# Linear attention on one core: queries, keys and values projected in one run, the gate's projection between the state's two chunks, the numerators last in a tile

## The reference

```
q = phi(rope(x @ Wq + bq)); k = phi(rope(x @ Wk + bk))      # 16 heads of 16; phi = elu + 1
v = x @ Wv + bv;            g = sigmoid(x @ Wg + bg)
for each chunk of 64 tokens:
    S = S + k_c^T v_c;      Z = Z + sum(k_c)
    out_c = g_c * (q_c S) / (q_c Z + 1e-6)
x = x + out @ Wo + bo                                        # x is rms-normed before the projections
```

## Time and profile before

| | |
|---|---|
| median of 3 runs | 1467.9 us (1464.53 to 1470.61) |
| profiled execution | 1477.02 us, its span 1475.2 us |
| PE busy in the span | 1422.5 us, 96% |
| PEld / DVE / ACT / POOL busy | 93% / 68% / 49% / 53% |
| mean granted TensorE clock | 0.976 |
| attention phase in the trace | 0 to about 226 us |

### The profile page before, as it was taken

How to read it: one execution, slowest core, us unless ns; L and a number is a source line. 1 busy time by engine, 2 the same in 40 slices (tenths; PEclk the granted TensorE clock), 3 DMA queues, 4 the chain that set the end, 5 groups by cost and what they waited for, 6 DMA issues and landing times. The chain is left out here.

```text
span 1475.2 us, 36261 instructions
## 1 busy us (share of the span) xinstructions
PE 1422.5 (96%) x11761; PEld 1373.3 (93%) x11761; DVE 1008.9 (68%) x2860; ACT 717.1 (49%) x1793; POOL 776.7 (53%) x792
## 2 busy tenths in 40 slices
PE   8999995999999999999969999999999999999997
PEld 7888884999999999999958999999999999999997
DVE  6999986666677667667685656666566656566685
ACT  4776664555555545555553434444344434443353
POOL 3677751566666666666442444344443444343477
PEclk9999996999999999999978999999999999999999
DMA  7121223343343442443443142313323132321442
GB/s 269 44 72 41 66 72 86 97 106 52 94 102 49 105 102 43 101 101 76 88 173 111 29 122 36 115 29 75 75 33 117 29 114 36 114 36 29 114 146 86
DMA packets 63560, 124.79 MB, mean 85 GB/s; under 512 B 14336, under 2 KB 51840, under 8 KB 60416
## 3 DMA queue, kind: packets, MB, share of 16 engines
q0 software_dynamic: 35936, 47.89, 18.9%
q1 hardware_dynamic: 27552, 76.02, 14.2%
HBM read 80.97 MB, written 42.90 MB: 84 GB/s over the span
## 5 line engine op out<-in xcount | busy, mean ns | idle before, releaser
L926 POOL DMA_INDIRECT mg<-meta,IDX x160 | 151.0, 944 | 307.0 <-DVE E_gate L1278 280.6
L1364 DVE TENSOR_TENSOR E_hraw<-E_sg,bank 128x256 f32<-128x256 f32 x320 | 133.2, 417 | 242.1 <-ACT E_sg L1212 191.7
L1061 POOL DMA_INDIRECT acc<-ysb,IDX x150 | 241.5, 1610 | 77.6 <-issue 48.6
L1434 PE MATMUL bank<-E_xT,ws 128*128 128x256 f32 x960 | 267.6, 279 | 3.9 <-ACT E_hraw L1215 2.5
L1435 PE MATMUL bank<-E_xT,ws 128*128 128x256 f32 x960 | 265.6, 277 | 0.0
L1436 PE MATMUL bank<-E_xT,ws 128*128 128x256 f32 x960 | 265.6, 277 | 0.0
L1375 DVE TENSOR_TENSOR E_hT<-E_hraw,E_hT 128x256 fp32r<-128x256 f32 x640 | 259.9, 416 | 0.0
L1371 DVE CAST E_hT<-E_hraw 128x256 fp32r<-128x256 f32 x640 | 203.1, 318 | 78.7 <-ACT E_hraw L1215 72.2
L1212 ACT ACTIVATE E_sg<-bank 128x256 f32<-128x256 f32 x320 | 116.0, 382 | 240.0 <-PE bank L1436 228.7
L1434 PEld LDWEIGHTS bank<-E_xT,ws 128*128 128x128 f32 x960 | 180.5, 188 | 7.6 <-ACT E_hraw L1215 5.3
L1434 PE MATMUL bank<-ws,E_hT 128*128 128x256 f32 x640 | 180.6, 282 | 0.0
(11 more groups left out here) (238 smaller groups left out, 3938.8 us busy)
## 6 DMA issues: line engine op xcount, KB each, us to landing
wraw<-in_w_ffn SPq DMA_DIRECT2D x8, 3072.0 KB, 10.8
wraw<-in_w_moe SPq DMA_DIRECT2D x8, 2048.0 KB, 12.2
acc<-x SPq DMA_DIRECT2D x32, 128.0 KB, 1.7
xn<-xn SPq DMA_DIRECT2D x32, 128.0 KB, 1.7
acc<-X POOLq DMA_DIRECT2D x4, 1024.0 KB, 9.0
acc<-X SPq DMA_DIRECT2D x8, 512.0 KB, 4.2
X<-acc SPq DMA_DIRECT2D x7, 512.0 KB, 5.9
X<-in_x SPq DMA_DIRECT2D x3, 1024.0 KB, 11.9
```

Of the source, the lines that this page charges most:

```text
L926: nc.gpsimd.indirect_dma_start(out=mg[:, j, 0:width], out_offset=None, in_=rows, in_offset=bass.IndirectOffsetOnAxis(ap=IDX[:, u * UT + j: ...
L1061: nc.gpsimd.indirect_dma_start(out=acc_dram, out_offset=at_slots(u, j), in_=ysb[:, j, :], in_offset=None, compute_op=ALU.add).then_inc(s_y ...
L1364: V.tensor_tensor(hraw[:, f % RING, :], sg[:, f % RING, :], bank[f % RING][:, UW:2 * UW], ALU.mult).then_inc(s_hm, 1)
L1434: nc.tensor.matmul(out, wh, mh, start=first, stop=False)
```

## The change

Only the order of blocks in TensorE's `step` changes, with each block's own waits. Every instruction, operand, bank and semaphore count is the same, and the other engines' programs are as before.

- before: P0, turn, tq, S0, V, S1, to, G, num, wo
- after: P0, V, turn, tq, to, S0, G, S1, wo, num

```diff
@@ TensorE's step
                     project(n, b_p0[:, :], half_a).then_inc(s_pj0, 1)
+                if (n := at(1)) is not None:
+                    if n == 0:
+                        pe.wait_ge(s_wl, 3 * KD)
+                    after(pe, s_vf, n)
+                    project(n, b_pv[:, 0:D], slice(2 * D, 3 * D)).then_inc(s_pjv, 1)
                 if (n := at(2)) is not None and n:
                     turn(n)
...
                     ins.then_inc(s_tq, 1)
-                    pe.wait_ge(s_vz, 2 * n + 1)
-                    after(pe, s_mk, 2 * n)
-                    add_chunk(n, 0)
-                if (n := at(1)) is not None:
-                    if n == 0:
-                        pe.wait_ge(s_wl, 3 * KD)
-                    after(pe, s_vf, n)
-                    project(n, b_pv[:, 0:D], slice(2 * D, 3 * D)).then_inc(s_pjv, 1)
-                if (n := at(0)) is not None:
-                    pe.wait_ge(s_mk, 2 * n + 1)
-                    pe.wait_ge(s_vz, 2 * n + 2)
-                    add_chunk(n, 1)
                 if (n := at(-1)) is not None:
                     pe.wait_ge(s_og, n + 1)
                     after(pe, s_oT, n)
...
                     ins.then_inc(s_to, 1)
+                if (n := at(0)) is not None:
+                    pe.wait_ge(s_vz, 2 * n + 1)
+                    after(pe, s_mk, 2 * n)
+                    add_chunk(n, 0)
                 if (n := at(1)) is not None:
                     after(pe, s_gt, n)
                     after(pe, s_lx, n)
                     project(n, b_pg[:, 0:DX], slice(3 * D, WX)).then_inc(s_pjg, 1)
+                if (n := at(0)) is not None:
+                    pe.wait_ge(s_mk, 2 * n + 1)
+                    pe.wait_ge(s_vz, 2 * n + 2)
+                    add_chunk(n, 1)
                 if t == -1:
                     turn_weights()
+                if (n := at(-1)) is not None:
+                    pe.wait_ge(s_oT, n + 1)
+                    pe.wait_ge(s_qT, min(n + 2, NT))
+                    after(pe, s_x1, n)
...
                     ins.then_inc(s_num, 1)
-                if (n := at(-1)) is not None:
-                    pe.wait_ge(s_oT, n + 1)
-                    pe.wait_ge(s_qT, min(n + 2, NT))
-                    after(pe, s_x1, n)
...
```

More of the change, by code:

```diff
@@ L647, in step @@
                     project(n, b_pg[:, 0:DX], slice(3 * D, WX)).then_inc(s_pjg, 1)
+                if (n := at(0)) is not None:
+                    pe.wait_ge(s_mk, 2 * n + 1)
+                    pe.wait_ge(s_vz, 2 * n + 2)
+                    add_chunk(n, 1)
                 if t == -1:
                     turn_weights()
+                if (n := at(-1)) is not None:
+                    pe.wait_ge(s_oT, n + 1)
+                    pe.wait_ge(s_qT, min(n + 2, NT))
+                    after(pe, s_x1, n)
+                    for k in range(KD):
+                        ins = nc.tensor.matmul(wo_ps, oT[:, k, :], wo[:, k, :], start=(k == 0), stop=(k == KD - 1))
+                    ins.then_inc(s_wo, 1)
                 if (n := at(0)) is not None:
@@ L660, in step @@
                     ins.then_inc(s_num, 1)
-                if (n := at(-1)) is not None:
-                    pe.wait_ge(s_oT, n + 1)
-                    pe.wait_ge(s_qT, min(n + 2, NT))
-                    after(pe, s_x1, n)
-                    for k in range(KD):
-                        ins = nc.tensor.matmul(wo_ps, oT[:, k, :], wo[:, k, :], start=(k == 0), stop=(k == KD - 1))
-                    ins.then_inc(s_wo, 1)
             run_tiles(pe, step)
```

## The result

The changed kernel takes 1477.3 us in the median of 7 runs, 1467.9 before; the ratio is 1.0074 with a 95% interval of 1.0053 to 1.0096. A second series (`after_again`), beside runs of its own of the kernel before, gave 1476.8 against 1464.8, ratio 1.0087 (1.0065 to 1.0109). So it is slower by 0.5 to 1.1%. The forecast was 1476.0 us, +8.1.

What follows compares the result with a forecast made beforehand. TensorE was taken as the bound, with small waits. Tile 6.12 + 0.54 = 6.66 us against 6.41, +0.25; 30 tiles give 7.5, with the end 8.1; 1467.9 + 8.1 = 1476.0 us, range 1465 to 1483.

Steps and rivals of the forecast that it cites:

- G's wait on the copy: In each attention tile, TensorE's G waits for ScalarE's copy of 8 logit columns: +0.54 us (0.38 to 0.72).
- The 0.15 from copy to matmul: From the logit copy's end to G's first matmul, a wait on two semaphores, taken as 0.15 us.
- What the new order takes away: In each attention tile, TensorE loses waits of 0.16 and 0.12 and another 0.02: 6.12 us without any new wait.
- two waits of TensorE (0.16 and 0.12): Old order, per tile: S1's wait on mask 0 with a bare load, 0.16 us; num's second half behind mask 1, 0.12.
- The first rival: G finds the logit copy done: tile 6.12 us, whole kernel 1459.8 us, faster; chance 0.1.
- The third rival: ScalarE falls behind in the attention tiles, slower still: 1480.5 to 1484 us; chance 0.15.
- Phi: At the start of VectorE's step: its move was put at nothing, with some 0.5 us to spare before mask 0.
- The ends: Start and end of the attention phase: 0 us (-0.8 to +0.8) and +0.6 us (0 to 0.8).
- The weight loads: On TensorE, loads are hidden behind matmuls in flight, bare after a wait (0.10 us); the skill's rule would give 3 us more.

Runs made afterwards that it cites:

- e11: The kernel before with tq and S0 moved ahead of turn (the input's transposes): 1469.0 us against 1464.8, ratio 1.0028.
- e4: The kernel before with only wo and num swapped at the tile's end: 1477.8 us against 1464.7, ratio 1.0096.

## Why the prediction was right, step by step

- **G's wait on the copy.** Right in mechanism, place and size. Forecast: S0 at 2.85 after P0, G at 3.79, tile 6.66, +0.25; measured 2.86, 3.80, 6.68 and +0.27. Moving the copy earlier took the wait away, moving it later lengthened the tile, and in the old order an early copy was worth nothing.
- **The 0.15 from copy to matmul.** It was 0.14, and 0.06 with G's two waits written in the other order.
- **What the new order takes away.** Right for this kernel, wrong as a floor. S1 and num wait for no mask there only because G's wait gives the masks time; without that wait S1's bare load is back, and the quiet tile is 6.27, not 6.12. I had added up two waits of TensorE (0.16 and 0.12) as if each were worth its length. In the old order one loop through both engines set the tile: S1's wait lay beside it, and when e11 took that away, num waited longer for mask 1.
- **The first rival** would therefore not have been 1459.8: with the copy out of the way the kernel still took 1468.3, 0.3% more than before.
- **The third rival**, ScalarE behind, did not decide here, but it does as soon as the copy is early.
- **Phi.** I put VectorE's move at nothing, with "some 0.5 us to spare". The tile bears this out in the whole change, though phi took up to 1.10 there and left mask 0 a wait of only 0.34 to 0.44 us in the tiles read; without V ahead of tq the tile was 0.35 longer than before (e4). Phi's own growth to 1.10 I had not seen.
- **The ends.** Mis-sized. For the start I took 0 and it was +1.3; for the end +0.6, and it was +1.5, both at full clock. With the 7.8 of the tiles that is 10.6 us where 8.1 were forecast; the two series gave 9.4 and 12.1 between medians. That the forecast of 1476.0 came within 1.3 us of the first series is therefore in part luck.
- **The weight loads.** The bare load after a wait was seen at S1 in the old order and gone in the new (0.57 to 0.47), so loads do pass matmuls in flight here, against the rule of the Trainium skill's page "TensorE: Matmul & The Clock Gate", section "What overlaps and what doesn't". The 0.10 went with the wait, and the 3 us more of that rule did not come.

## What to carry to other kernels

When blocks of an in-order engine are moved, follow each block's results through the other engines' own orders to whoever frees the next buffer; an eight-column copy behind three larger operations held a block back by 0.56 us in each tile here. Before adding up an engine's small waits, look for the loop that sets the period, through all its engines: a wait beside it is worth nothing, and a move that shortens one link can lengthen the next, as e11's did. Judge a change in a repeated stage by its steady tiles, which repeat to 0.1%, and keep the stage's ends apart, with the granted clock of each end beside its time.

## What was unexpected of the hardware

- VectorE's phi (128x512) and GpSimd's multiplication into `A_og` (128x256) lengthen each other by who starts first. In the 14 profiles they ran side by side for 0.4 us or more 292 times between 25 and 215 us: `A_og` first gave phi 0.97 to 1.11 us and left `A_og` its 0.62; phi first gave phi 0.63 to 0.73 and `A_og` 0.88 to 1.09.
- Of two waits ahead of one weight load, the one that comes as a separate instruction (0.05 us long in the trace) cost 0.08 us more than the one on the load itself (0.14 against 0.06 from the copy's end to the matmul).
- The same program kept the full clock through the start of the phase in one execution and had a mean of 0.63 over 14 us in another; it was worth 3 us.
